# Graph attention on one core: edges sorted in two sets, the second inside the loop over the first, with the table made in pairs of blocks

## The reference

```python
recv, send = src, dst
wn_out = x[send] @ W_lin + b_lin
e_ij = leaky_relu2(concat([x[recv], x[send]]) @ W_att + b_att)   # slope 0.2
a_ij = (e_ij @ w_alpha)[:, 0]
a_exp = exp(a_ij - segment_max(a_ij, recv)[recv])
alpha = a_exp / max(segment_sum(a_exp, recv)[recv], 1e-12)
n_i = elu(segment_sum(alpha[:, None] * wn_out, recv))
out = layernorm(x + n_i)
```

## Time and profile before

| what | us |
|---|---|
| median of 3 runs (2672.36 to 2678.7) | 2672.62 |
| the profiled execution's own time | 2676.63 |
| its span, first to last instruction | 2674.9 |
| DVE's first comparison of the sort | 34.47 |
| start of the first gather | 517.46 |
| start of the last gather | 2598.36 |

### The profile page before, as it was taken

The page is one execution under the profiler, slowest core; times in us unless marked ns, Lnnn a source line. Parts: engine busy times, 40 slices in busy tenths (PEclk is TensorE's granted clock), DMA queues, the critical chain, the costliest instruction groups (busy, mean ns, idle before and its releaser), DMA issues.

```text
span 2674.9 us, 67073 instructions
## 1 busy us (share of the span) xinstructions
PE 2265.2 (85%) x13543; PEld 1535.4 (57%) x13752; DVE 1938.0 (72%) x4727; ACT 1338.6 (50%) x4146; POOL 1584.3 (59%) x1674
## 2 busy tenths in 40 slices
PE   3991211199999999999999999999999999999981
PEld 1330111166666666666666666666666666666661
DVE  7978999866666666666666666666666666666667
ACT  3772111055555555555555555555555555555545
POOL 0000000277777777777777777777777777777760
PEclk9998555599999999999999999999999999999996
DMA  4110000043333333333333333333333333333361
GB/s 103 39 41 19 0 0 0 22 108 105 105 106 104 105 105 104 106 105 105 106 104 105 105 104 106 105 105 106 105 105 105 104 105 106 104 106 105 105 93 50
DMA packets 96368, 235.57 MB, mean 88 GB/s; under 512 B 27935, under 2 KB 41205, under 8 KB 96135
## 3 DMA queue, kind: packets, MB, share of 16 engines
q0 software_dynamic: 79744, 218.60, 31.3%
q1 hardware_dynamic: 16594, 16.65, 2.2%
HBM read 225.32 MB, written 9.82 MB: 88 GB/s over the span
## 4 chain that ended last, share of the span: by engine, by line
PE 80%; DVE 11%; issue 4%; DMA 2%; POOL 2%; ACT 1%; DVEq 0%; SPq 0%; POOLq 0%; ACTq 0%
PE hidden_ps L675 24%; PE turned_ps L702 14%; PE masked_ps L686 14%; PE turned_ps L693 8%; PE hidden_ps L672 8%; DVE keys_i L900 4%; DVE keys_i L899 4%; PE turned_ps L660 3%; PE hidden_ps L615 3%; PE hidden_ps L614 2%; PE masked_ps L685 2%; POOL rows L412 2%; DMA rows<-qv_table,index 1%; DMA x_sb<-in_x 1%; PE masked_ps L608 1%
## 5 line engine op out<-in xcount | busy, mean ns | idle before, releaser
L412 POOL DMA_INDIRECT rows<-qv_table,index x1660 | 1576.1, 949 | 557.5 <-issue 476.5
L531 ACT ACTIVATE keys_i<-masked_ps,peaks 128x128 f32<-128x128 f32 x1660 | 474.5, 368 | 602.4 <-DVE peaks L1028 602.4
L675 PE MATMUL hidden_ps<-onehotT,p_part 128*128 128x128 bf16 x4980 | 740.4, 220 | 1.4
L1020 DVE TENSOR_REDUCE unit_low<-masked_ps 128x4 f32<-128x512 f32 x415 | 287.1, 692 | 594.8 <-PE masked_ps L686 594.8
L675 PEld LDWEIGHTS hidden_ps<-onehotT,p_part 128*128 x4980 | 472.2, 96 | 275.5 <-issue 205.1
L702 PEld LDWEIGHTS turned_ps<-rows,keys_i 128*128 128x128 f32 x3320 | 456.8, 190 | 299.5 <-issue 269.3
L1049 DVE SCALAR_TENSOR_TENSOR sums<-sums,shrink,turned_ps 128x129 f32 x1660 | 572.5, 345 | 66.3 <-issue 2.9
L702 PE MATMUL turned_ps<-rows,keys_i 128*128 128x129 f32 x3320 | 523.0, 280 | 15.1 <-issue 11.6
L672 PE MATMUL hidden_ps<-identf,rows 128*128 128x128 f32 x1660 | 470.4, 283 | 15.7 <-DMA rows<-qv_table,index 10.7
L686 PE MATMUL masked_ps<-leaky,w_cols 128*128 128x512 f32 x830 | 424.9, 593 | 10.9
L522 ACT ACTIVATE keys_i<-hidden_ps 128x512 f32<-128x512 f32 x415 | 247.9, 597 | 319.7 <-PE hidden_ps L675 319.5
(11 more groups left out here) (133 smaller groups left out, 1618.5 us busy)
## 6 DMA issues: line engine op xcount, KB each, us to landing
rows<-qv_table,index POOLq DMA_INDIRECT x1660
qv_table<-qv_out SPq DMA_DIRECT2D x49, 128.5 KB, 2.3
out<-x_sb SPq DMA_DIRECT2D x1, 1344.0 KB
recv_mem<-unit_blocks SPq DMA_DIRECT2D x1, 896.0 KB, 5.2
out<-x_sb SPq DMA_DIRECT2D x1, 896.0 KB
keys_i<-in_src SPq DMA_DIRECT2D x1, 768.0 KB
keys_i<-in_dst SPq DMA_DIRECT2D x1, 768.0 KB
recv_mem<-in_src SPq DMA_DIRECT2D x1, 604.5 KB
```

Source lines behind the costliest of these rows:

```text
L412: g.indirect_dma_start(out=rows[:, j % U, c, :], out_offset=None, in_=table, in_offset=bass.IndirectOffsetOnAxis(ap=index[:, j % U, c:c + ...
L531: last = a.activation(weightsT[:, j % 2, unit], masked_ps[:, j % 2, unit], ACT.Exp, bias=peaks[:, bass.ds(k * PER + i + 1, 1)])
L675: mm = t.matmul(whole[:, unit], p_parts[s][:, bass.ds(of[c // SUB], F)], onehotT[:, j % 4, unit], start=False, stop=(s == 2), skip_group_c ...
L1020: v.tensor_reduce(unit_low[:], masked_ps[:, j % 2, :].rearrange("p (i e) -> p i e", i=PER), AX_X, ALU.max, negate=True).then_inc(unit_low_ ...
```

## The change

**Two sets.** The row width falls from 2048 to `W` = 1024. The first set has `E_A` = 121 x 1024 = 123904 edges and 7 rows of pads; the second has the other 82346 edges. The first is cut into `NA` = 254 chunks, the second into 173: 427 together, from 415. Only the first set is sorted ahead of the loop, by the same scheme with 10 stages for 11 inside a row (`LOCAL`).

**Second sort.** `second_sort` is a generator that yields after every stage. 11 steps of it run on DVE between the runs of the first sort (`FILLING`), and one behind the last `add_sums` of every chunk, up to chunk 179 or so: 188 steps with 26 empty ones (`GAP`). Its transposes (`aside_run`, four of 128 x 128 each) go through `weights_ps`, PE's between other work of the chunk and ACT's copies too. ACT makes 24 of the 49 counts of the second set behind the runs of the first sort and 25 inside the first 25 chunks. The first 256 chunks are unrolled on PE, DVE and ACT; POOL's loop stays rolled over 8 chunks.

**Boundary.** At chunk 251 the last peak of every block in the first set is carried over: transposes of the peaks, a sum of 8 matmuls against `last_of`, two matmuls that spread it over the second set's units, ACT's copies between them.

**Table.** Two blocks share one round between PE and ACT; the bias comes as three bf16 rows, and the split in three bf16 parts is made by PE matmuls with minus the identity into the same PSUM tile, in place of `split_p`. Five pairs go beside the counts, five behind them, fifteen behind the runs (`TABLE_BEHIND`). `x - 1` moves from the front into the loop.

**Scan.** The scan runs over 8 elements a chunk for 4, each peak paired with a `lows` entry; `shrink` is computed without the ReLU. `fresh` is bf16.

**Padding of the first set.** One comparison of 128 x 2744 and one reduction in place of the 49 steps of L855; the second set keeps the 49 steps.

```diff
-    WIDTH = 2048
+    W = 1024
+    EDGE_ROWS = [P - PROWS, 0]
+    E_A = EDGE_ROWS[0] * W
+    NA = UNITS_A // PER
+    NCH = NA + NBC
+    UNROLLED = -(-NA // U) * U
+    COUNTS_A_WITH = {15: 0, 22: 1, 29: 2, 36: 3, 43: 4}
+    TABLE_BEFORE = [5, 6, 7, 8, 9]
+    TABLE_BEHIND = {1: [10, 11], 3: [12, 13], 5: [14, 15], 6: [16], 7: [17, 18], 8: [19], 9: [20, 21], 10: [22], 11: [23, 24]}
+    COUNTS_BEHIND = {1: 3, 3: 3, 5: 3, 7: 3, 9: 3, 11: 3, 12: 6}
+    FILLING = {1: 2, 2: 2, 3: 1, 4: 1, 5: 1, 7: 1, 9: 1, 11: 1, 13: 1}
...
@@ scalar
+            def table_pair(g):
+                n = min(2, NB - 2 * g)
+                act.wait_ge(pqv_ps, g + 1)
+                copy_part(g, 0)
+                if g >= 2:
+                    act.wait_ge(qv_stored[g % 2], g // 2 * 16)
+                a.activation(qv_out[:, g % 2, 0:n, 0:ONES], pair_ps[g % 2][:, 0:n, F:3 * F], ACT.Copy).then_inc(qv_ready, 1)
+                act.wait_ge(p_less, 2 * g + 1)
+                copy_part(g, 1)
+                if g % 2 == 0 and g // 2 + 1 < QUADS:
+                    copy_xT(g // 2 + 1)
+                act.wait_ge(p_less, 2 * g + 2)
+                copy_part(g, 2)
...
@@ tensor
+            def project(g):
...
+                for n in range(min(2, NB - 2 * g)):
+                    whole = pair_ps[g % 2][:, n, 0:3 * F]
+                    at = (2 * g + n) % 4 * P
+                    t.matmul(whole, xT[:, g // 2 % 2, at:at + P], w3[:], start=True, stop=False, skip_group_check=True)
+                    mm = t.matmul(whole, onesb[:], bias_parts[:], start=False, stop=False, skip_group_check=True)
+                mm.then_inc(pqv_ps, 1)
...
+            def table_pair(g):
+                if g % 2 == 0 and g // 2 + 1 < QUADS:
+                    turn_x(g // 2 + 1)
+                if g + 1 < PAIRS:
+                    project(g + 1)
+                lessen_p(g, 0)
+                lessen_p(g, 1)
...
+            def aside_run(run, h):
+                if h == 0:
+                    pe.wait_ge(run_done[1], run + 1)
+                pe.wait_ge(aside_out, aside_of_run(run, h) - 1)
+                for c in range(C):
+                    at = h * PIECE + c * P
+                    mm = t.transpose(weights_ps[:, c * P:(c + 1) * P], keys[1][:, ends_in[run], at:at + P], identf[:])
+                mm.then_inc(aside_ps, 1)
...
@@ vector
+            def second_sort():
...
+                for phase in range(1, LOCAL):
+                    for stage in reversed(range(phase)):
+                        if done:
+                            dve.wait_ge(compared[1], done)
+                        for r in (0, 1):
+                            compare_groups(keys[1][sorting, now, :], keys[1][sorting, 1 - now, :], 1 << stage,
+                                           1 << phase, r).then_inc(compared[1], 1)
+                        done, now = done + 2, 1 - now
+                        yield
...
+                        elif phase == PHASES:
+                            last = compare(src, dst, 1 << (phase - LOCAL - 1 - n))
...
             def step(i, j):
...
-                if PER > 2:
-                    add_sums(k, j, 3, of)
-            chunks(dve, step)
+                add_sums(k, j, 3, of)
+                if unrolled and chunk_of(steps) == k <= LANES_AT + 1:
+                    second_on(1)
+            chunks(dve, step, UNROLLED)
```

More of the change, by code:

```diff
@@ L9 @@
 I32 = mybir.dt.int32
-U16 = mybir.dt.uint16
 ALU = mybir.AluOpType
@@ new lines, in lessen_p @@
+            def lessen_p(g, part):
+                pe.wait_ge(part_ready, 3 * g + part + 1)
+                if part == 0:
+                    pe.wait_ge(qv_ready, g + 1)
+                for n in range(min(2, NB - 2 * g)):
+                    at = (2 * g + n) * F
+                    mm = t.matmul(pair_ps[g % 2][:, n, 0:F], minusb[:], p_parts[part][:, at:at + F], start=False,
+                                  stop=(part == 1), skip_group_check=True)
+                mm.then_inc(p_less, 1)
@@ new lines, in table_pair @@
+            def table_pair(g):
[5 more added lines that the diff above has]
+                lessen_p(g, 1)
+            turn_x(0)
+            project(0)
+            for b in sorted(COUNTS_A_WITH):
+                table_pair(COUNTS_A_WITH[b])
+            pe.wait_ge(signed[0], NB + 1)
+            t.matmul(totals, onesf[:], signs[0][:], start=True, stop=True).then_inc(totals_ps, 1)
@@ L699, in unit_sums @@
                     pe.wait_ge(sums_ready, (k - 1) * PER + end)
-                for i in range(first, end):
-                    for c in range(i * SUB, (i + 1) * SUB):
-                        mm = t.matmul(unit_sums_ps[:, i, :], weights[:, j % 2, c * P:(c + 1) * P],
-                                      rows[:, j % U, c, F:R], start=(c == i * SUB), stop=(c == (i + 1) * SUB - 1))
+                for c in range(first, end):
+                    mm = t.matmul(unit_sums_ps[:, c, :], weights[:, j % 2, c * P:(c + 1) * P],
+                                  rows[:, j % U, c, F:R], start=True, stop=True)
                 mm.then_inc(done, 1)
@@ L746, in _ @@
+            chunks(pe, step, UNROLLED)
         @block.vector
@@ L912, in _, with second_on @@
+            second, steps = second_sort(), 0
+            def second_on(count):
+                nonlocal steps
+                for n in range(count):
+                    next(second)
+                    steps += 1
             done, now = 0, 0
-            edge_rows = slice(0, EDGE_ROWS)
             for phase in range(1, LOCAL):
                 if done:
-                    dve.wait_ge(compared, done)
+                    dve.wait_ge(compared[0], done)
                 for stage in reversed(range(phase)):
@@ L934, in within @@
                 small = LOCAL - 1
-                dve.wait_ge(compared, done)
-                compare(keys[rows, now, :], keys[rows, 1 - now, :], PIECE).then_inc(compared, 1)
+                dve.wait_ge(compared[0], done)
+                compare(keys[0][rows, now, :], keys[0][rows, 1 - now, :], PIECE).then_inc(compared[0], 1)
                 now, done = 1 - now, done + 1
@@ L939, in within @@
                 for n in range(small + LEAD):
-                    if n == LEAD + 2 and between:
-                        between()
+                    if n == LEAD + 4 and between:
+                        for part in between:
+                            pass
                     for h, stage in ((0, n), (1, n - LEAD)):
@@ L953, in within @@
                 return done
-            done = within(edge_rows, now, done, between=make_padding)
+            done = within(edge_rows, now, done, between=padding(0))
             for run in range(1, RUNS):
                 phase, now = phase_of(run), starts_in[run]
+                second_on(FILLING.get(run, 0))
+                if run == 7:
+                    pack_blocks(0)
+                    find_fresh(0)
                 if run % 2:
```

1104 lines of the change are left out of this document (670 added, 434 removed).

## The result

The changed kernel takes 2547.12 us (median of 4 runs, 2544.81 to 2549.24), the kernel before beside it 2673.31 (2672.36 to 2678.7): a ratio of 0.9524, 95% interval 0.9507 to 0.954. The forecast was 2540 in 2485 to 2610. The profiled execution took 2547.15 with a span of 2545.2, so it stands at the median; the granted clock was 0.946 on average.

What follows compares the result with a forecast made beforehand. POOL's gather issuing was taken to bound the loop. First gather at 276, gathers 2141.1, held gathers 45, behind the last gather 76.5 make a 2538.6 us span; with 1.7 around it, 2540 us, range 2485 to 2610.

Steps and rivals of the forecast that it cites:

- The frame: Loop: POOL's gather issuing sets the pace, 1.2543 us per gather, 2141.1 us over 1707 intervals.
- The front: Everything ahead of the first gather: sorting on DVE, first gather at 276 us, 241 earlier than before.
- run 0: Front: stretch of the first set's sort on DVE, eight half stages behind the padding, ending at 102 us.
- table delay: Front, sort runs: table pairs and counts on ACT and PE delay DVE by about 5 us in all.
- The hold: Loop: gathers starting inside a DVE comparison of two SBUF tensors wait until it has ended, 45 us in all.
- if each comparison frees it, the mean is half a comparison: Loop: a held gather goes on at its own comparison's end; 0.17 over 66 chunks, 0.30 over 96, 40 us.
- The cover: Loop: extra work on PE, ACT and DVE is hidden by the 8 slots of rows; taken as 0 us.
- The end: Behind the last gather's start: 76.5 us, as in the kernel before.
- no hold: Loop rival: comparisons hold no gather, POOL keeps 1.2543 throughout; 2495 us, chance 0.20.
- Through the whole step: Loop rival: a gather is held to the end of the whole comparison step, 97 us; 2592 us, chance 0.20.
- held by gathers: Loop rival: DVE's comparisons also wait for gathers, 280 us, making the change slower; 2775 us, chance 0.04.
- The table: Front rival: late counts and table pairs on ACT set the front, 40 of 45 us bound; 2580 us, chance 0.12.

Runs made afterwards that it cites:

- z1_reduce: Changed kernel with each second-sort comparison in the loop replaced by a tensor_reduce of one SBUF operand, second set left unsorted; 2480.42 us, ratio 0.9279.
- z2_first: Changed kernel with all comparisons of a step in one series behind the chunk's first add_sums instead of the fourth, complete result; 2511.37 us, ratio 0.9396.
- y4_between: Changed kernel with a step's comparisons split behind the chunk's first and second add_sums, at most two in a row, complete result; 2510.76 us, ratio 0.9389.
- y1_tiny: Changed kernel with the second sort's comparisons in the loop working on one column each, second set left unsorted; 2484.28 us, ratio 0.9286.
- z4_front: Changed kernel with 18 small half stages of the first sort's six even runs on two columns, first set not sorted rightly; 2510.58 us, ratio 0.9404.
- x1_tiny: Changed kernel with the loop's comparisons on one column each, run where the kernel before took 3751.58 us; 3596.74 us, ratio 0.9581.

## Why the prediction was right, point by point

The sum was 276 + 2141.1 + 45 + 76.5 + 1.7; measured, in the same terms, it is 273.9 + 2133.7 + 58 + 79.5 + 1.9.

1. **The frame** held: POOL's spacing set the loop before and after, and POOL waited for no engine. The spacing behind the sort was 1.250, not 1.2543, 7 us over all gathers.
2. **The front**: 273.9 against 276, with errors that cancel; that it came out within 2 is luck. The first comparison started at 14.68 (14.5 forecast). The counts, with "nothing to spare", were late: a pass took 1.27 with its read and not 1.12, and DVE stood 3.5 us at `totals`. The padding's two instructions took 3.01 each, not 3.35, but it ended at 101, not 97; run 0 ended at 106.7 (102), and run 1 started at 109.4 (106). From there to the senders, at 272.0, it took 162.6, where 163 and 5 of table delay were forecast: the delay didn't come, and made up for the late start.
3. **The hold**: it exists, at its place and as "held until the comparison has ended"; z1_reduce shows that it goes with the comparisons. This term was mis-sized: 40 for the comparisons and 5 for the rest, measured 56.3 and 2. The step that failed is "if each comparison frees it, the mean is half a comparison". 82 gathers were freed so and lost 19.4 us; 47 were held to the end of the step, the other bound of the price, and lost 36.9, 28 more than their own comparisons' ends would have cost. The two bounds were right, and neither was the truth: the chip does both. Freed at its own comparison each, all would have lost 28 and not 40, for two reasons: the steps beside gathers are 139 (59 of four instructions and 80 of two) and not 162, and a gather loses only what is left over 0.13 us. Two errors thus went one way and the larger one the other. A last thing the step left out is that gather starts aren't spread evenly over the chunk: with the same number of comparisons the holds were 9 to 56 us by place alone.
4. **The cover** held where I had put 0: PE's extra turns, the boundary, the unrolled code, the small pad steps. The measure is z1_reduce, which has all of them and loses 3 us in the loop. It is not so wherever the comparisons stand: in z2_first POOL did wait for PE.
5. **The end**: 79.5 for 76.5. The last rows landed 13.7 us behind their gather for 11.4, PE ended 15.6 behind that for 15.2, and what follows PE took 50.3 for 49.9. So most of the 3 us is the DMA engines' delay over the pads; why it is 2 us longer than before is open. The clock isn't the reason: over the 20 us behind the last gather it was 0.90 granted here and 0.91 before, and y4_between, with 1.00 there, ended 79.1 behind its last gather all the same.
6. **The rivals**: no hold would have been 2495, and z1_reduce and y1_tiny give 2480 and 2484: of y1_tiny's profiled 2479.5, 8 us less are the pads that it leaves unsorted, 6 the gathers at 1.250, 2 the front. Through the whole step, 2592, fell, though 47 of 129 gathers did just that. DVE's comparisons of 512 weren't held by gathers: 153 of 160 took 0.67 to 0.69 beside them, as in front of the first gather, and none over 0.72. The table did not set the front, but z4_front shows it next in line.

## What to carry to other kernels

Where GpSimd's issuing sets the pace, look at what DVE does beside it. Of as many columns in the same place, reductions of one SBUF operand cost nothing and comparisons of two cost 56 us, 2%. But the number of operands is not the test, since `tensor_scalar` of one SBUF operand held gathers too: read how long a gather takes beside each kind of instruction. If such instructions are needed, don't put them in one series at the end of the chunk. Moving them was worth 35 us here (2511 for 2547). In pieces behind several `add_sums` they left the pace to POOL; in one series behind the first, DVE and PE set it at 5.08 us a chunk in place of 5.00, for the same time in the end. And price a front by what comes second: of 57 us cut from DVE, 26 came back as waits for ACT.

## What the runs showed of the hardware

- A gather that starts inside a comparison of two SBUF operands, over 0.13 us ahead of its end, ends 0.80 to 0.83 us behind the end of that comparison or of the last one of the same unbroken series; the longest took 2.23 us for 0.95. In z2_first 50 gathers that started less than 0.03 us behind a comparison of 512 weren't held, and the comparison took 0.73 to 0.75 for 0.68.
- `tensor_scalar` of one SBUF operand held gathers in the same way: 1.95 across L1131 and L1132 of z1_reduce, 1.16 and 1.17 at L1138 and L1218. So did the pads' `scalar_tensor_tensor` of two SBUF operands at L1068, wherever 0.14 to 0.17 us of it were left (0.96 to 0.99, 3 in the changed kernel and 5 in z1_reduce). `tensor_reduce` of one SBUF operand left gathers at 0.95 (136 in z1_reduce), and so did, but for one gather, the instructions with a PSUM operand. That one, of 1.85 us, started inside L1326, 0.44 ahead of the `tensor_scalar` L1124; it isn't explained. The scan at L1361 left them at 0.95 as well, but it lasts 0.22 us, so a hold could hardly show.
- 128 rows side by side, gathered again and again, take 0.73 of the DMA engines for 81 GB/s, 0.90 per 100 GB/s; eight rows apart 0.40 per 100, and mixed with all others 0.39 (0.41 at 106). At the end of the changed kernel their last rows land 13.7 us behind the gather that fetched them, mixed rows 2.6.
- The same program, y1_tiny and x1_tiny, took 2484 and 3597 us with the same number of gathers, and the kernel before 2673 and 3752. In x1_tiny the granted clock was 0.82 for y1_tiny's 0.95, and PE waited 859 us in sum for ACT at L846, while the first gather, at 273.8 in both, and the front were as fast.
